# A time-warp stage whose tables move in row blocks, and an integer stage with three batches in flight

## What is computed

```python
def _dtw_cost(D):
    row0 = jnp.cumsum(D[0])
    def row_step(prev_row, d_row):
        first = d_row[0] + prev_row[0]
        def col_step(left, inp):
            d_ij, up, diag = inp
            r = d_ij + jnp.minimum(jnp.minimum(up, left), diag)
            return (r, r)
...
def _align_one(small, large):
    D = _pairwise_euclidean(small, large)
    R = _dtw_cost(D)
    i_idx, j_idx, valid = _backtrack(R, T_small, T_large)
    contrib = small[i_idx] * valid[:, None].astype(small.dtype)
    expanded = jnp.zeros((T_large, d), dtype=small.dtype).at[j_idx].add(contrib)
...
def _xla_quantized_matmul(x2d, weight_q, weight_scale):
    amax = jnp.max(jnp.abs(x2d), axis=-1, keepdims=True)
    x_scale = jnp.maximum(amax, EPS) / 127.0
    x_q = jnp.clip(jnp.round(x2d / x_scale), -128, 127).astype(jnp.int8)
    acc = jax.lax.dot_general(x_q, weight_q, (((1,), (1,)), ((), ())), preferred_element_type=jnp.int32)
    return acc.astype(jnp.float32) * x_scale * weight_scale[None, :]
```

## Time and profile before

| what | value |
|---|---|
| median of three runs | 1896.55 us |
| the profiled execution: its own time, and its span from first to last instruction | 1886.68 us, 1884.7 us |
| busy share of the span: PE, DVE, ACT, POOL | 73%, 66%, 30%, 18% |
| time-warp stage, from its first load to the next stage's first load | 770.86 to 996.56 us |
| integer stage, to the end of its last DVE operation | 996.56 to 1100.28 us |

### The profile page before, as it was taken

How to read it: one execution, slowest core, us unless ns; L and a number is a source line. 1 busy time by engine, 2 the same in 40 slices (tenths; PEclk the granted TensorE clock), 3 DMA queues, 4 the chain that set the end, 5 groups by cost and what they waited for, 6 DMA issues and landing times. The chain is left out here.

```text
span 1884.7 us, 32009 instructions
## 1 busy us (share of the span) xinstructions
PE 1382.4 (73%) x9677; PEld 1160.8 (62%) x9677; DVE 1237.1 (66%) x3141; ACT 560.5 (30%) x1628; POOL 343.5 (18%) x484
## 2 busy tenths in 40 slices
PE   3668999999999966100002359999789899979998
PEld 2337888888888855100001137777678699868887
DVE  5875776677776757696595748888645466535554
ACT  2331212112221113000000017777423576623232
POOL 4750000000000001000001114444323111122221
PEclk9668999999999985555555569999889999989999
DMA  5541212112121124202307227777422111100000
GB/s 186 172 144 30 57 29 53 31 29 56 29 51 33 29 74 125 46 0 37 75 0 215 78 80 180 192 193 187 105 62 67 49 51 50 35 22 17 22 17 17
DMA packets 176323, 137.73 MB, mean 73 GB/s; under 512 B 16818, under 2 KB 170243, under 8 KB 173892
## 3 DMA queue, kind: packets, MB, share of 16 engines
q1 hardware_dynamic: 158864, 119.75, 24.5%
q10 hardware_dynamic: 17396, 17.23, 3.2%
HBM read 100.87 MB, written 36.06 MB: 73 GB/s over the span
## 5 line engine op out<-in xcount | busy, mean ns | idle before, releaser
L720 DVE TENSOR_TENSOR moa_oe<-moa_mask,moa_ogT 128x1024 fp32r<-128x1024 bf16 x128 | 155.4, 1225 | 35.7 <-PE moa_k_ps L93 32.6
L1142 PE MATMUL warp_t_ps<-ident,warp_entry 128*128 128x128 f32 x1 | 0.5, 477 | 220.8 <-DVE warpb_hit L1125 220.8
L91 PE MATMUL moa_k_ps<-moa_w_out_hi,moa_oe 128*128 128x256 f32 x512 | 150.2, 293 | 13.6 <-DVE moa_oe L720 13.6
L92 PE MATMUL moa_k_ps<-moa_w_out_lo,moa_oe 128*128 128x256 f32 x512 | 143.8, 281 | 0.0
L93 PE MATMUL moa_k_ps<-moa_w_out_hi,moa_oe 128*128 128x256 f32 x512 | 143.4, 280 | 0.0
L1142 PEld LDWEIGHTS warp_t_ps<-ident,warp_entry 128*128 128x128 f32 x1 | 0.2, 183 | 221.1 <-DVE warpb_hit L1125 221.1
L1851 PE MATMUL L_b_ps<-L_v,L_pT 128*128 128x128 f32 x1024 | 127.3, 282 | 1.4 <-DVE L_xo L1538 0.8
L1851 PEld LDWEIGHTS L_b_ps<-L_v,L_pT 128*128 128x128 f32 x1024 | 121.9, 197 | 6.8 <-issue 6.8
L91 PEld LDWEIGHTS moa_k_ps<-moa_w_out_hi,moa_oe 128*128 128x128 f32 x512 | 96.9, 189 | 22.7 <-issue 16.9
L1681 ACT ACTIVATE L_xnT<-L_b_ps 128x256 f32<-128x256 f32 x16 | 5.8, 365 | 352.0 <-PE L_b_ps L1773 352.0
L687 DVE COPY_PREDICATED moa_v_sel<-moa_onehot,moa_y_ps 128x512 f32<-128x512 int32 x112 | 82.2, 734 | 40.0 <-DVE moa_v_sel L687 29.8
(11 more groups left out here) (334 smaller groups left out, 3780.4 us busy)
## 6 DMA issues: line engine op xcount, KB each, us to landing
bounce<-L_rel SPq DMA_DIRECT2D x64, 258.0 KB, 4.1
moa_mask<-chosen SPq DMA_DIRECT2D x32, 512.0 KB, 5.9
L_shifted<-bounce SPq DMA_DIRECT2D x64, 256.0 KB, 4.3
ret_staged_values<-in_w_value_dram ACTq DMA_DIRECT2D x8, 512.0 KB, 3.7
ret_staged_outputs<-in_w_out_dram ACTq DMA_DIRECT2D x8, 512.0 KB, 4.0
ret_cT<-in_ctxT_pairs_dram SPq DMA_DIRECT2D x16, 256.0 KB, 2.8
L_x<-x_after SPq DMA_DIRECT2D x32, 128.0 KB, 2.2
L_cT<-in_ctxT_pairs_dram SPq DMA_DIRECT2D x32, 128.0 KB, 2.7
```

The lines of the kernel that those rows point to most:

```text
L91: pe.matmul(out, x_hi, w_hi, start=first, stop=False)
L92: pe.matmul(out, x_hi, w_lo, start=False, stop=False)
L720: dve.tensor_tensor(oe[e % 2][:, :, :, :].rearrange("p a m s -> p a (m s)"), mask[:, e, :, :].rearrange("p m s -> p (m s)").unsqueeze(1).t ...
```

## The change

In the time-warp stage:

- `dd` is loaded in three blocks of rows (0 to 8, 8 to 40, 40 to 128), each with its own semaphore, and the first row waits for the first block.
- The cost table is stored in four blocks (0 to 64, 64 to 104, 104 to 120, 120 to 128) as soon as their rows are done, and each is read back into `cost` and `above` (which now live through both blocks) while later rows are computed.
- `steps` is stored in three blocks, the last 16 rows first, and each is read back into `chase` once written; the lookups wait block by block.
- `path` is an SBUF tensor. The last scan writes it, its store is gone, and the integer stage's p is copied from SBUF to SBUF.

In the integer stage `in_deep_phases` (L110) takes the place of `in_two_phases`. In a step b the engines work on batches b to b+3: PE makes the alignment product of b+3; DVE normalizes b+1, adds b+2, quantizes b+1 and scales the product of b. The order on each engine is written out below. The gate is multiplied into the weight scales and the bias once, ahead of the batches. The result of a batch is `scaled` (DVE) + `xab` (POOL) on POOL, where `xab` = `xa` + gated bias is a POOL operation too. The quantized values stay f32 (`int_clipped`, transposed with the f32 identity), and ACT copies the transpose to SBUF as bf16, taking the rounding constant off. ACT's copies stand behind its 23 weight loads.

```diff
-                    sp.dma_start(dd[:, :, :].rearrange("b i j -> b (i j)"), dist.rearrange("b i j -> b (i j)")).then_inc(dist_in, 16)
+        LOADS = ((0, 8), (8, 40), (40, S))
+        COSTS = ((0, 64), (64, 104), (104, 120), (120, S))
+        STEPS = ((112, S), (64, 112), (0, 64))
+                    for (r0, r1), landed in zip(LOADS, dist_in):
+                        sp.dma_start(dd[:, r0:r1, :], dist[:, r0:r1, :]).then_inc(landed, 16)
...
-                    sp.wait_ge(row_ready, after(S))
-                    sp.dma_start(costs[:, 1:S + 1, :].rearrange("b i j -> b (i j)"), rr[:, :, :].rearrange("b i j -> b (i j)")).then_inc(costs_out, 16)
+                    for (r0, r1), written in zip(COSTS, costs_out):
+                        sp.wait_ge(row_ready, after(r1))
+                        sp.dma_start(costs[:, r0 + 1:r1 + 1, :], rr[:, r0:r1, :]).then_inc(written, 16)
+                        sp.wait_ge(written, after(16))
+                        sp.dma_start(cost[r0:r1, :, :], costs[:, r0 + 1:r1 + 1, :].rearrange("b i j -> i b j")).then_inc(tables_in, 16)
+                        sp.dma_start(above[r0:r1, :, :], costs[:, r0:r1, :].rearrange("b i j -> i b j")).then_inc(tables_in, 16)
+                    sp.wait_ge(tables_in, after(32 * len(COSTS)))
...
+                    for (r0, r1), written in zip(STEPS, steps_out):
+                        sp.dma_start(steps[:, r0:r1, :].rearrange("b i j -> i b j"),
+                                     nxt[r0:r1, :].rearrange("p (b j) -> p b j", j=S)).then_inc(written, 16)
+                    for (r0, r1), written, landed in zip(STEPS, steps_out, steps_in):
+                        sp.wait_ge(written, after(16))
+                        sp.dma_start(chase[:, r0:r1, :], steps[:, r0:r1, :]).then_inc(landed, 16)
...
-                    sp.dma_start(path.rearrange("i b j -> i (b j)"), nxt[:, :]).then_inc(steps_out, 16)
...
-                    sp.dma_start(p[v][:, :], path[:, bass.ds(n, 1), :].rearrange("i a j -> i (a j)")).then_inc(in_loaded[v], 16)
+                    sp.dma_start(p[v][:, :], path[:, bass.ds(n * S, S)]).then_inc(in_loaded[v], 16)
...
+                    if ahead and (not isinstance(b, int) or b + 4 < B):
+                        sp.wait_ge(xa_ready, after(b + 3))
+                        load(b + 4, u)
+                    if middle:
                         sp.wait_ge(xo_ready, after(b + 1))
                         sp.dma_start(x_out[b], xo[u][:, :]).then_inc(x_stored[u], 16)
...
+                    if middle:
+                        pool.wait_ge(xab_ready, after(b + 1))
+                        pool.wait_ge(scaled_ready, after(b + 1))
+                        pool.wait_ge(x_stored[u], stores(b, u))
+                        pool.tensor_tensor(xo[u][:, :], scaled[:, u, :], xab[:, u, :], ALU.add).then_inc(xo_ready, 1)
...
+                    if front:
+                        act.wait_ge(qT_ps, after(b + 2))
+                        act.wait_ge(acc_done, after(b + 1))
+                        act.activation(qT[:, :, :], t_ps[:, 0:D].rearrange("p (t s) -> p t s", s=S), ACT.Identity,
+                                       bias=minus_round[:, :]).then_inc(qT_ready, 1)
...
+                    if front:
+                        pe.wait_ge(step_done, after(b * 5 + 10))
+                        pe.wait_ge(qT_ready, after(b + 1))
                         for t in range(DT):
+                            last = pe.transpose(t_ps[:, 128 * t:128 * t + 128], clipped[:, 128 * t:128 * t + 128], k.ident[:, :])
                         last.then_inc(qT_ps, 1)
```

More of the change, by code:

```diff
@@ L1071, in row @@
                                                dd[:, i, :], BIG, ALU.min, ALU.add).then_inc(row_ready, 1)
-                    for i in range(1, S):
-                        row(i, i % 2)
+                    for (r0, r1), landed in zip(LOADS, dist_in):
+                        dve.wait_ge(landed, after(16))
+                        for i in range(max(r0, 1), r1):
+                            row(i, i % 2)
         with ExitStack() as bulk_ctx:
             sbb = lambda n, s, t=F32: bulk_ctx.enter_context(nc.sbuf_tensor("warpb_" + n, s, t))
-            cost, above = sbb("cost", [128, B, W]), sbb("above", [128, B, W])
             low = sbb("lowb", [128, B, S])
@@ L1090, in _ @@
                 def _(sp):
-                    sp.dma_start(cost[:, :, :], costs[:, 1:S + 1, :].rearrange("b i j -> i b j")).then_inc(tables_in, 16)
-                    sp.dma_start(above[:, :, :], costs[:, 0:S, :].rearrange("b i j -> i b j")).then_inc(tables_in, 16)
                     sp.wait_ge(bulk, after(7))
[L1094 to L1097, removed]
-                    sp.dma_start(path.rearrange("i b j -> i (b j)"), nxt[:, :]).then_inc(steps_out, 16)
-                    sp.wait_ge(steps_out, after(32))
+                    for (r0, r1), written in zip(STEPS, steps_out):
[4 more added lines that the diff above has]
+                        sp.dma_start(chase[:, r0:r1, :], steps[:, r0:r1, :]).then_inc(landed, 16)
+                    for landed in steps_in:
+                        sp.wait_ge(landed, after(16))
                 @block.vector
@@ L1226, in step @@
[L1226 to L1236 removed]
+                        ln.normalize(dve, n, xa[:, nu, :])
@@ L1256, in _, with expand @@
+                dve.tensor_scalar(scaled_weight[:, :], w_scale[:, :], k.gates[:, 5:6], None, ALU.mult).then_inc(setup, 1)
+                dve.tensor_scalar(gated_bias[:, :], bias[:, :], k.gates[:, 5:6], None, ALU.mult).then_inc(setup, 1)
+                step(-2, 0, front=False, middle=False, tail=False)
+                in_deep_phases(dve, step)
             @block.tensor
             def _(pe):
-                def step(b, u, front=True, main=True):
+                def expand(n, v):
+                    pe.wait_ge(in_loaded[v], loads(n, v, 3))
+                    pe.wait_ge(xa_ready, after(n))
+                    pe.matmul(e_ps[:, 0:D], p[v][:, :], c[v][:, :], start=True, stop=True).then_inc(expanded, 1)
@@ L1259, in step @@
+                def step(b, u, ahead=True, front=True, middle=True, tail=True):
                     nu = 1 - u
+                    if ahead and (not isinstance(b, int) or b + 3 < B):
+                        expand(b + 3, nu)
                     if front:
-                        pe.wait_ge(in_loaded[nu], loads(b + 1, nu, 3))
-                        pe.wait_ge(xa_ready, after(b + 1))
-                        pe.matmul(e_ps[:, 0:D], p[nu][:, :], c[nu][:, :], start=True, stop=True).then_inc(expanded, 1)
@@ L1277, in step @@
                         last.then_inc(acc_done, 1)
-                in_two_phases(pe, step)
+                expand(0, 0)
+                step(-2, 0, front=False, middle=False, tail=False)
+                pe.wait_ge(weights_cast, after(1))
+                in_deep_phases(pe, step)
 def sinusoid_reversed_T():
@@ L2460, in build @@
         dist, costs = scratch("dist", (B, S, S)), scratch("costs", (B, S + 1, S + 1))
-        steps, path = scratch("steps", (B, S, S)), scratch("path", (S, B, S))
+        steps, path = scratch("steps", (B, S, S)), sb("path", [128, B * S])
         stage_distances(k, x_in, dist, L2_weights)
```

129 lines of the change are left out of this document (65 added, 64 removed).

## The result

The changed kernel takes **1836.97 us** (median of four runs, 1836.52 to 1839.53) where the kernel before, run beside it, took 1896.34 (1895.06 to 1896.75): a ratio of 0.9691, 95% interval 0.9674 to 0.9708, 59.4 us less by the medians. The forecast was 1841.4, the range 1828 to 1857. The profiled execution takes 1836.6 us, its span is 1834.8.

A forecast was written before the change was run, and what follows sets the result against it. The prediction took the time-warp stage's serial chain with transfer waits and, in the integer stage, DVE's list as the bounds. Savings of 36.5 and 18.7 us sum to 55.2, taken off 1896.55 for 1841.4 us; range 1828 to 1857.

The forecast's parts named there:

- first load: Time-warp stage: a small first block of dd lets DVE start 2.6 us behind the load's issue, saving 9.1 us.
- table out and back: Time-warp stage: cost-table blocks move under rows, leaving a 7.0 us wait instead of 21.3, saving 14.3 us.
- steps out and back: Time-warp stage: the wait ahead of the first lookup falls from 16.55 to 7.4 us, saving 9.1, bounds 7 and 11.
- path's store: End of the time-warp stage: the store goes, the engines' meetings stay, saving 4.0 us.
- integer stage: Whole integer stage: 85.0 us instead of 103.7 at 4.2 us per batch, saving 18.7 us, bounds 9 and 29.
- DVE's own list: Integer stage: DVE's own work per batch falls from 5.85 to 3.4 us, before POOL's effect is added.
- POOL's term: Integer stage: one POOL operation per batch holds DVE, 0.73 us and a little, making the batch 4.2 us.
- The rival of two collisions: Integer stage: POOL holds DVE for both additions and part of the root, 5.0 to 5.7 us per batch, about 1856 us; 20%.
- The deeper pipeline brings nothing: Integer stage: step stays at 5.85 us because ACT's hop lies on the chain; kernel 1863 us; 5%.
- loads decide: Integer stage: slow load landings make the kernel slower than before; at 15 us landing, 1905 us; 2%.
- no collision: Integer stage: POOL's additions do not hold DVE, 3.4 us per batch, kernel 1831 us; 15%.
- The blocks pay their fixed time on the chain: Time-warp stage: 14 added transfers cost 2.0 us each, 28 us, kernel 1869 us; 7%.

The follow-up runs named there:

- e6: Changed kernel with larger blocks: first dd load 40 rows instead of 8, last cost-table block 32 rows instead of 8; 1838.66 us, 0.9753 of the kernel before.
- e5: Changed kernel with the first block of steps read back before the other two are stored; 1827.67 us, 0.9689 of the kernel before.
- e3: Changed kernel with POOL's two additions cut to one column of 256; 1820.09 us, 0.9624 of the kernel before.
- e4: Changed kernel with ACT's 23 weight loads issued behind its copies of the transposes, not ahead of the first; 1820.62 us, 0.9638 of the kernel before.
- e7: Changed kernel with POOL's two additions moved right behind int_xa, none left out, store one step later; 1821.57 us, 0.9654 of the kernel before.
- e2: Kernel before with only the integer stage changed, path still in HBM; 1867.27 us, 0.9884 of the kernel before.

## Why the prediction was right

| term | forecast, us saved | measured | |
|---|---|---|---|
| first load | 9.1 | 9.0 | right in size; the last wait is POOL's fill |
| table out and back | 14.3 | 14.9 | right; e6 shows its rate |
| steps out and back | 9.1 | 7.7 | 8.87 in place of the 7.4 put; inside its bounds |
| path's store | 4.0 | 4.0 | right |
| integer stage | 18.7 | 21.6 | step 3.88 in place of 4.2 |
| sum | 55.2 | 57.2 | 56.9 by the stages' lengths, 59.4 by the medians |

**The first load.** The number came out partly by luck. The block landed 2.2 us behind its issue where 2.6 was put, and POOL's fill, which the forecast did not look at, ended at 2.6. The wait of before was not for `dd` alone either: its row names `iota_j`, issued 0.41 us behind `dd`, and the changed kernel waits for that only ahead of the wide operations.

**The steps.** The mechanism was named (the read stands behind the other stores); its size was put too low. The read was given 1.3 us of data and some 2 us behind the stores' end at 4 us; the third store landed 6.8 us after its issue, and the read took 5.8. e5 gives 2.6 for it without those stores.

**The integer stage.** Its gain is 2.9 us above the forecast, and nearly all of that lies in the step: from the first `int_scaled` to the 14th 50.8 us in place of 54.6, with a start 0.6 us later and an end 0.3 longer. The term that was mis-sized is DVE's own list, put at 3.4 us; e3 shows 2.95 to 3.2. The 3.4 came out of the mean of two batches, 5.65 and 6.05 us; the longer one held a stand of 0.29 us ahead of `int_xa` that the forecast did not look at. This is the row, from DVE's timeline of the kernel before:

```profile
1057.13 0.48 DVE L1222 SCALAR_TENSOR_TENSOR int_xa<-int_e_ps,gates,int_x 128x256 f32<-128x256 f32 x1 [0.29 <-issue]
```

The shorter batch alone gives 5.65 - 2.45 = 3.2 by the same subtraction. POOL's term came out in size, by luck: it was put at one collision of 0.73 us and a little, and the trace has two, which cost 0.7 to 0.9 us together. Each holds DVE only from the end that its operation would have had alone to 0.15 us behind POOL's end, and `int_xo` is already 0.17 us old when `int_clipped` comes. The forecast left open whether `int_ln_xn` "meets `int_xab` or goes ahead of it" and put one operation for each batch; from the second step on it meets it in each. The rival of two collisions had the count right and the time wrong: it priced each at POOL's full 0.73 us, added part of the root, beside which `int_shifted` keeps its 0.35 us, and set all this on a list that was too long.

The first `int_scaled` came at 22.4 us, as forecast (21.8), though the reason given was not the whole: the loads, slow beside the weights, had part in it (e4). The second came 4.4 us later: in that step POOL's additions stretched `int_shifted` and `int_clipped`, and DVE waited 0.35 us for PE.

**The rivals.** "The deeper pipeline brings nothing" and "loads decide" fall by the step, "no collision" by the rows of the step and by e3. "The blocks pay their fixed time on the chain" falls by the stage's 35.3 us and by e6: larger blocks at two places cost 5.6 us. The Trainium skill's page "DMA: Bandwidth & Descriptors" (Rules for kernel authors) wants small transfers joined; here the 64 KB blocks landed in 1.9 and 2.2 us and the larger ones later, and DVE waited only for the landing of the first block of a load or a read-back and of the last block of the table. By the price that the forecast set beside that rule, the kernel would have taken 1869 us.

The Trainium skill's "GPSIMD Engine Reference" (Key points) puts POOL's contention on DVE's operations in a two-port mode or with two SBUF inputs. The traces agree as far as they go: in e7 `int_scaled`, which reads PSUM and one SBUF tile, keeps 0.48 us beside POOL's addition, and `int_amax` and the statistics keep their own times; the operations that stretch read one f32 tile of SBUF and write another, and which mode they run in no row shows.

## What to carry to other kernels

Between two stages that hand a table through HBM, cut the transfer so that the block on the chain is small, and look at what stands ahead of that block on its queue, not at the block alone. When work moves to POOL, list which DVE operations will stand beside it: here f32 operations from SBUF to SBUF paid until POOL's addition was done, reductions and reads of PSUM paid nothing, so POOL's work was best placed beside the latter. An engine that has become a link of the chain should not have a row of weight loads ahead of its first step.

## What the runs showed of the hardware

- POOL may be held too: its inverse root, 0.55 us in most steps of e3, took 0.69 in most steps of the changed kernel, where `int_shifted` began 0.30 us after it. But in e7 it took 0.55 again in most steps, whether `int_shifted` began with it or 0.37 us after it; what decides it no run tells.
- While ACT's weight loads moved, with about 300 GB/s in all, p's 64 KB took 5.2 us to land in place of 2.0; spread over the stage (e4) they left it at 2.9 and the step at 3.9.
- p from SBUF to SBUF lands no sooner than p from HBM: 2.0 us for both, and the same step in e2.
- Stores out of `rr` beside DVE's rows cost the rows nothing: 97.2 against 97.0 us.
